# Second layer's scores as products of 64 rows, two heads in the two row halves of the array

## The chip, the cores and the metric

The kernel runs on one core of a Trainium2 chip. The metric is the device time of one execution in microseconds (us). The engines are TensorE (PE, its weight loads are PEld), VectorE (DVE), ScalarE (ACT), GpSimd (POOL) and SyncE (SP), which here only issues transfers.

## The reference

Two layers, each an attention over 77 context rows and a linear feed-forward, on x of 8 batches x 512 tokens x 512. What matters here is the attention of the second layer, with 16 heads of 64:

```python
q = jnp.einsum('bsd,dhe->bshe', inputs_q, Wq) + bq
k = jnp.einsum('bsd,dhe->bshe', inputs_kv, Wk) + bk
v = jnp.einsum('bsd,dhe->bshe', inputs_kv, Wv) + bv
q = q / jnp.sqrt(jnp.asarray(HD, dtype=q.dtype))
scores = jnp.einsum('bqhd,bkhd->bhqk', q, k)
weights = jax.nn.softmax(scores, axis=-1)
ctx = jnp.einsum('bhqk,bkhd->bqhd', weights, v)
out = jnp.einsum('bqhd,hde->bqe', ctx, Wo) + bo
```

with inputs_q the layer-normalised x (512 tokens), inputs_kv the context (77 rows), D = 512 and HD = 64. The first layer is alike with 16 heads of 32, a key mask and no output matrix. Its feed-forward has ternary weights and quantised rows; the second layer's is one real 512 x 512 matrix made in setup from two DFT products.

## The kernel before, in words

**Numbers.** Every operand of a product is held as a sum of two fp16 parts, high and low. `products` (L150 to L152) makes three matmuls of each product: high x high, high x low, low x high.

**Two programs.** `setup` (0 to about 191 us of the profile) scales and splits all weights and computes keys and values of all batches, which go to DRAM (`scr_k0`, `scr_v0`, `scr_k1`, `scr_v1`). The weights come through two staging buffers, `stage[:, 0]` and `stage[:, 1]`, filled by `load(i, n)` on the SP queue in the order of `STAGED`; each load waits until the weight before it in its buffer is split. VectorE runs a chain in one fixed order over them (`maximum`, `scaling`, `low`), among it the waits for `WO` and for `WV1A` and `WV1B`, the two halves of the second layer's value weights. Small vectors, the value bias `vb1` among them, are counted on one semaphore, `small_in`.

`layers` is one loop over steps i of 18 slots each; a step works on all four stages of neighbouring batches. W and X are the query projection, attention and feed-forward of the first layer, Y the second layer's query projection and attention, Z its output product and feed-forward: `("X", u)` and `("Y", u)` in `UNITS` are the eight score units of a batch and a layer. A unit is 128 tokens x 8 heads. `FILLS` says which other products ("fills": projections `q`, probabilities x values `pv`, output `out`, feed-forward `f`) TensorE makes in each slot into one of four banks `wb`. TensorE's order is written out: in slot g it makes the scores of the unit of slot g + 1, then the fills of slot g (for Y's unit 0 the fills come first). So a step has Y units 0 and 1 back to back; 2 behind a few fills; 3, 4 and 5 back to back, as two slots between them have no fills; then 6 and 7, each behind fills. Behind unit 5 stands the first projection of the next batch, `("W", "q", 0)`, 12 matmuls of 512 columns.

**A score unit's way.** Scores go to `sc[:, U % 2]`, two banks of 4 heads x 77 columns; units alternate between two pairs of banks. VectorE takes the maxima (L1135, `maxima`). In the units of `HEADWISE` ScalarE makes the exponentials head by head from the bank (L981, eight heads of 0.42 us and less); in the others VectorE subtracts the maxima (L1143) and ScalarE makes one pass (L985). GpSimd normalises, ScalarE and VectorE split into high and low (L994, L1155), and a transposing DMA on the SP queue turns the probabilities for `pv`. TensorE waits before unit U until the exponentials (or the subtraction) of unit U - 2 are done (L1210 and on, `scores`).

**Y's scores.** Queries of two heads, 2 x 64 rows, are one 128-row stationary operand `qc[:, h, pair, tok]`. The keys `k1b[rows, h, pair, j, :]` hold head j of the pair in rows 64 j to 64 j + 63 and zeros in the other half, so that one matmul over 128 rows and 2 x 77 = 154 columns gives both heads: the zeros take out the other head's rows. A unit is 4 pairs x 3 = 12 such matmuls. The one matmul of another row count in the loop is `ones` x `mrow` (L1223), one row, which adds the mask in every bank of an X unit.

Of the kernel before, what the change touches and what calls it, by code (L numbers as in the profile page):

```python
# [13 lines left out]
P = 128  # L14
B, S, D = 8, 512, 512
KEYS = 77
ROWS = B * KEYS
NT = S // P
ND = D // P
H0, H1 = 32, 64  # L20
D1 = 16 * H1
ND1 = D1 // P
# [208 lines left out]
def setup(nc, k, ctxT, wk0, bk0, wv0, bv0, wk1, bk1, wv1, bv1, scr_k0, scr_k1, scr_v0, scr_v1,  # L231
# [4 lines left out]
    with here:  # L236
# [3 lines left out]
        def sem(name):  # L240
            return here.enter_context(nc.semaphore(name))

        stage = sb("a_stage", [P, 2, ND * ROWS], F32)
# [40 lines left out]
        STAGED = [[("WF", wf[:, 0:ND * D], ND * D), ("WQ0", wq0, ND * D), ("WK0", wk0, ND * D), ("WK1A", wk1[:, :, 0:D], ND * D),  # L284
                   ("WV1B", wv1[:, :, D:D1], ND * D)],
                  [("WF", wf[:, ND * D:2 * ND * D], ND * D), ("CTX", ctxT, ND * ROWS), ("WV0", wv0, ND * D),
                   ("WV1A", wv1[:, :, 0:D], ND * D), ("WK1B", wk1[:, :, D:D1], ND * D)]]
        W_PLACE = {"WK0": 0, "WV0": 1, "WK1A": 0, "WK1B": 1, "WV1A": 1, "WV1B": 0}
# [41 lines left out]
        def _(sp):  # L330
            def load(i, n):
                name, src, width = STAGED[i][n]
                if n:
                    sp.wait_ge(lo_done, split_count(STAGED[i][n - 1][0]))
                o = stage[:, i, 0:width]
                if len(src.shape) == 3:
                    o = o.rearrange("p (c n) -> p c n", c=ND)
                sp.dma_start(o, src).then_inc(loaded[i], 16)
# [12 lines left out]
            sp.dma_start(vb0, bv0.partition_broadcast(P)).then_inc(small_in, 16)  # L351
            sp.dma_start(vb1, bv1.partition_broadcast(P)).then_inc(small_in, 16)
            sp.dma_start(k["bo"][:, :], bo.partition_broadcast(P)).then_inc(small_in, 16)
# [6 lines left out]
            sp.wait_ge(tern_full, ND)  # L360
            sp.dma_start(wo_ks[:, 0:ND1 * D], wo).then_inc(wo_in, 16)
            load(1, 2)
# [28 lines left out]
        def _(dve):  # L391
            step = Chain(dve, dve_step)

            arrival = {name: (loaded[i], 16 * (n + 1)) for i in range(2) for n, (name, _, _) in enumerate(STAGED[i])}
            arrival["WQ1"], arrival["WO"] = (wq1_in, 16), (wo_in, 16)
            biased = {"WQ0": k["bq0"], "WQ1": k["bq1"]}
# [118 lines left out]
            ternary()  # L515
            dve.wait_ge(small_in, 16 * 11)
            mask_rows()
# [89 lines left out]
        def _(act):  # L607
# [44 lines left out]
            for name in ("WK0", "WO", "WV0"):  # L652
                high(name)
            act.wait_ge(small_in, 16 * 11)
            k_factor(S_WK0, 0)
# [86 lines left out]
def layers(nc, k, x, scr_k0, scr_k1, scr_v0, scr_v1, out):  # L742

    here = ExitStack()
    with here:
# [437 lines left out]
        def _(pe):  # L1183
# [21 lines left out]
            def scores(stage, u, b):  # L1205
# [12 lines left out]
                tok = slice(t * P, (t + 1) * P)  # L1218
                for gg in range(2):
                    g = 2 * half + gg  # L1220
                    if stage == "X":
                        o = sc[:, U % 2, gg, 0:GK]
                        pe.matmul(o.rearrange("p (h n) -> p h n", h=4), ones[:, :], mrow[:, :, :].broadcast_to([1, 4, KEYS]), start=True, stop=False)  # L1223
                        ins = products(pe, o, lambda h: q0T[:, h, g, tok],
                                       lambda h: k0b[:, h, g, :, :].rearrange("p j n -> p (j n)"), False, True)
                    else:
                        for e in range(2):
                            pair = 2 * g + e
                            ins = products(pe, sc[:, U % 2, gg, e * 2 * KEYS:(e + 1) * 2 * KEYS], lambda h: qc[:, h, pair, tok],
                                           lambda h: k1b[:, h, pair, :, :].rearrange("p j n -> p (j n)"), e == 0, True, skip=True)  # L1230
                ins.then_inc(scores_full, 1)
# [149 lines left out]
```

## Time and profile before

| | |
|---|---|
| median of 3 runs | 1251.98 us (1246.87 to 1256.07) |
| the profiled execution: its own time | 1256.17 us |
| its span, first to last instruction | 1254.4 us |
| outside the span | 1.8 us |
| mean granted TensorE clock | 0.886 of full speed |
| TensorE matmuls busy | 998.0 us (80%) |
| VectorE busy | 959.6 us (77%) |
| ScalarE busy | 647.3 us (52%) |
| GpSimd busy | 401.0 us (32%) |

Setup takes the first 191 us or so, the loop the rest; a step in the middle of the loop takes about 115 us. Busy time of TensorE is the union of its matmuls, which overlap in the record, as each is drawn from its start to its end: the distance between two starts is what a matmul costs the engine, not its length. Idle time in brackets stands before an instruction, with what ended it.

### The profile page before, as it was taken

To read this page: it belongs to the slowest core of one execution; us is meant where nothing else is said; L and a number is where in the kernel's file an instruction comes from. 1 tells how busy PE (TensorE), PEld (TensorE's weight loads), DVE (VectorE), ACT (ScalarE), POOL (GpSimd) and SP (SyncE) were. 2 spreads that over 40 slices of the span, in tenths; PEclk is the share of its full clock that TensorE was granted. 3 is DMA by queue.
4 is the path that set the end of the run, shared out by engine and by line. 5 is a ranking of instruction groups with operands and counts; after the bars stand their busy time and mean duration, and the time that the engine had idled before them with its cause. 6 is when DMAs were issued, how large, how long until landed. Compare 5 with 4: busy or idle time off the path is not lost. (4 is left out here: it accounts for less than half of the span.)

```text
span 1254.4 us, 17113 instructions
## 1 busy us (share of the span) xinstructions
PE 998.0 (80%) x6020; PEld 501.3 (40%) x6020; DVE 959.6 (77%) x1740; ACT 647.3 (52%) x1658; POOL 401.0 (32%) x350
## 2 busy tenths in 40 slices
PE   3989940555686896899699969979996999589694
PEld 1446430232253344445344534444453445334341
DVE  5798874286879969987897899699979977954832
ACT  1334340353657637753864686377539645713701
POOL 0011004041433324523441444245234413521402
PEclk9999975756688799999799989998998999799797
DMA  8402232153555655665657555756755573560512
GB/s 336 167 34 76 108 118 91 34 128 68 89 115 101 106 103 98 116 128 105 109 103 154 82 115 102 139 98 120 128 109 111 97 128 69 95 119 17 100 52 67
DMA packets 374983, 132.83 MB, mean 106 GB/s; under 512 B 364753, under 2 KB 367345, under 8 KB 371442
## 3 DMA queue, kind: packets, MB, share of 16 engines
q1 hardware_dynamic: 374898, 131.74, 49.4%
q8 instruction: 48, 0.79, 0.3%
q14 instruction: 37, 0.30, 0.1%
HBM read 35.91 MB, written 16.11 MB: 41 GB/s over the span
## 5 line engine op out<-in xcount | busy, mean ns | idle before, releaser
L938 POOL TENSOR_TENSOR pr<-pr,sm 128x616 f32<-128x616 f32 x128 | 168.7, 1318 | 454.5 <-DVE sm L1150 454.5
L981 ACT ACTIVATE pr<-scores,mx,factor 128x77 f32<-128x77 f32 x512 | 204.3, 421 | 44.8 <-DVE mx L1138 44.8
L150 PE MATMUL wb<-xT,wq_hl 128*128 128x512 f16 x384 | 150.9, 393 | 68.4 <-DMA xT<-xh 68.4
L151 PE MATMUL wb<-xT,wq_hl 128*128 128x512 f16 x384 | 150.4, 392 | 0.0
L152 PE MATMUL wb<-xT,wq_hl 128*128 128x512 f16 x384 | 149.8, 390 | 0.0
L994 ACT ACTIVATE ph<-pr 128x618 f16<-128x618 f32 x128 | 92.8, 725 | 99.4 <-DMA prT<-ph 86.7
L150 PE MATMUL scores<-k1b,qc 128*128 128x154 f16 x256 | 62.0, 259 | 90.3 <-ACT pr L981 89.5
L1155 DVE SCALAR_TENSOR_TENSOR ph<-pr,ph 128x618 f16<-128x618 f32 x128 | 130.0, 1016 | 4.4 <-ACT ph L994 4.4
L929 POOL TENSOR_TENSOR rstd<-var,mhalf 128x2 f32<-128x2 f32 (+1 forms) x48 | 52.5, 1094 | 183.9 <-DVE var L1052 176.4
L981 ACT ACTIVATION_READ_ACCUMULATOR pr<-scores,mx,factor 128x1 f32 x512 | 107.9, 211 | 0.0
L1135 DVE TENSOR_REDUCE mx<-scores 128x8 f32<-128x616 f32 x128 | 101.3, 791 | 8.2 <-PE scores L152 8.2
L150 PE MATMUL wb<-wo_hl,qc 128*128 128x512 f16 x256 | 97.0, 379 | 3.0 <-DVE qc L1085 3.0
L152 PE MATMUL wb<-wo_hl,qc 128*128 128x512 f16 x256 | 97.0, 379 | 0.0
L151 PE MATMUL wb<-wo_hl,qc 128*128 128x512 f16 x256 | 97.0, 379 | 0.0
L1094 DVE SCALAR_TENSOR_TENSOR xr<-wb,factor,xr 128x512 f32<-128x512 f32 x48 | 35.8, 745 | 77.6 <-PE wb L152 77.6
L1078 DVE TENSOR_TENSOR xh<-xn,xh 128x1024 f16<-128x1024 f32 x48 | 73.4, 1530 | 25.1 <-ACT xn L1009 24.6
L1006 ACT ACTIVATE xh<-xr,shift,rstd 128x512 f16<-128x512 f32 x72 | 58.0, 814 | 56.2 <-POOL shift L931 33.6
L962 ACT ACTIVATE qc<-wb,bq_s 128x512 f16<-128x512 f32 x64 | 42.5, 688 | 82.6 <-PE wb L152 82.6
L150 PEld LDWEIGHTS wb<-xT,wq_hl 128*128 128x128 f16 x384 | 38.8, 101 | 114.1 <-issue 74.5
L1009 ACT ACTIVATE xn<-xr,shift,rstd 128x512 f32<-128x512 f32 x84 | 67.0, 812 | 11.6 <-POOL shift L931 10.3
L944 POOL TENSOR_TENSOR xr<-xr,bf_b 128x512 f32<-128x512 f32 x48 | 70.4, 1487 | 3.8 <-ACT xn L1009 3.8
L388 POOL PARTITION_ALL_REDUCE a_allmax<-a_absmax x16 | 15.9, 992 | 162.8 <-DVE a_absmax L406 94.1
(177 smaller groups left out, 2616.2 us busy)
## 6 DMA issues: line engine op xcount, KB each, us to landing
xr<-in_x SPq DMA_DIRECT2D x6, 1024.0 KB, 5.6
out_x<-xr SPq DMA_DIRECT2D x6, 1024.0 KB, 5.5
a_dft_kf<-in_dft SPq DMA_DIRECT2D x1, 3072.0 KB, 14.3
a_stage<-in_wk SPq DMA_DIRECT2D x3, 1024.0 KB, 5.6
a_stage<-in_wv SPq DMA_DIRECT2D x3, 1024.0 KB, 5.6
scr_v<-a_wq_vs SPq DMA_DIRECT2D x1, 2560.0 KB, 7.8
scr_k<-a_wo_ks SPq DMA_DIRECT2D x1, 2464.0 KB, 7.2
k1b<-scr_k SPq DMA_DIRECT2D x16, 154.0 KB, 6.7
```

Of the source, the lines that this page charges most:

```text
L150: pe.matmul(out, lhs(0), rhs(0), start=start, stop=False, **kw)
L151: pe.matmul(out, lhs(0), rhs(1), start=False, stop=False, **kw)
L152: return pe.matmul(out, lhs(1), rhs(0), start=False, stop=stop, **kw)
L938: pool.tensor_tensor(v, v, s, ALU.mult).then_inc(probs_ready, 1)
L944: ins = pool.tensor_tensor(xs(b)[:, t, :], xs(b)[:, t, :], k[bias][:, :], ALU.add)
L981: ins = act.activation(pr[U % 3][:, h // 4, cols], sc[:, U % 2, h // 4, cols], ACT.Exp, bias=mx[:, U % 4, h:h + 1], scale=k["factor"][:, f ...
L994: act.activation(ph[:, U % 2, 0, :, :, 0:CH], pr[U % 3][:, :, 0:GKP].rearrange("p g (c n) -> p g c n", c=3), ACT.Copy, scale=PS).then_inc( ...
L1006: ins = act.activation(xh[:, n % 2, t - pair, 0, :], xs(b)[:, t, :], ACT.Identity, bias=shift[:, j, t:t + 1], scale=rstd[:, j, t:t + 1])
L1009: ins = act.activation(xn[:, t - pair, :], xs(b)[:, t, :], ACT.Identity, bias=shift[:, j, t:t + 1], scale=rstd[:, j, t:t + 1])
L1078: dve.tensor_tensor(xh[:, n % 2, :, 1, :], xn[:, :, :], xh[:, n % 2, :, 0, :], ALU.subtract).then_inc(ln_lowered, 1)
L1135: step(dve.tensor_reduce(m, s, AX.X, ALU.max))
L1155: dve.scalar_tensor_tensor(out=ph[:, U % 2, 1, :, :, 0:CH], in0=pr[U % 3][:, :, 0:GKP].rearrange("p g (c n) -> p g c n", c=3), scalar=PS, ...
```

## The change

Y's scores become 24 matmuls of 64 rows and 77 columns a unit. A new argument `tile_position=(r * 64, 0)` puts the product in row half r of the array; the two halves hold different heads, and r = 0 and r = 1 write to two banks. The zero half of `k1b` is no longer read. A bank then holds four heads that are not four in a row in the old numbering, so values and output weights have to come in the same new order: `WV1A`, `WV1B` and the bias `vb1` are loaded in 8 pieces each in place of 1, and `WO` in 8 in place of 1, with the counts of the semaphores to match. All else in the loop stays as it is; nothing changes in the order of work on VectorE, ScalarE and GpSimd.

```diff
@@ setup: STAGED
-                   ("WV1B", wv1[:, :, D:D1], ND * D)],
+                   ("WV1B", wv1, ND * D)],
...
-                   ("WV1A", wv1[:, :, 0:D], ND * D), ("WK1B", wk1[:, :, D:D1], ND * D)]]
+                   ("WV1A", wv1, ND * D), ("WK1B", wk1[:, :, D:D1], ND * D)]]
@@ load
+                if name in ("WV1A", "WV1B"):
+                    a = name == "WV1B"
+                    o = o.rearrange("p (c b g r d) -> p c b g r d", c=ND, b=2, g=2, r=2)
+                    src = src.rearrange("p c (b r g a d) -> p c b r g a d", b=2, r=2, g=2, a=2)
+                    for b, g, r in itertools.product(range(2), range(2), range(2)):
+                        sp.dma_start(o[:, :, b, g, r, :], src[:, :, b, r, g, int(a), :]).then_inc(loaded[i], 16)
+                    return
@@ SP queue
-            sp.dma_start(vb1, bv1.partition_broadcast(P)).then_inc(small_in, 16)
+            vb1_v = vb1.rearrange("p (a b g r d) -> p a b g r d", a=2, b=2, g=2, r=2)
+            bv1_v = bv1.rearrange("(b r g a d) -> b r g a d", b=2, r=2, g=2, a=2)
+            for q, r in itertools.product(range(4), range(2)):
+                sp.dma_start(vb1_v[:, q // 2, q % 2, :, r, :], bv1_v[q % 2, r, :, q // 2, :].partition_broadcast(P)).then_inc(small_in, 16)
...
-            sp.dma_start(wo_ks[:, 0:ND1 * D], wo).then_inc(wo_in, 16)
+            wo_v = wo_ks[:, 0:ND1 * D].rearrange("p (f r e n) -> p f r e n", f=2, r=2, e=2)
+            wo_s = wo.rearrange("p (f e u n) -> p f e u n", f=2, e=2, u=2)
+            for f, r, u in itertools.product(range(2), range(2), range(2)):
+                sp.dma_start(wo_v[u * H1:(u + 1) * H1, f, r, :, :], wo_s[r * H1:(r + 1) * H1, f, :, u, :]).then_inc(wo_in, 16)
@@ VectorE of setup (ScalarE alike)
-            dve.wait_ge(small_in, 16 * 11)
+            dve.wait_ge(small_in, 16 * 18)
@@ TensorE: scores
-                    else:
-                        for e in range(2):
-                            pair = 2 * g + e
-                            ins = products(pe, sc[:, U % 2, gg, e * 2 * KEYS:(e + 1) * 2 * KEYS], lambda h: qc[:, h, pair, tok],
-                                           lambda h: k1b[:, h, pair, :, :].rearrange("p j n -> p (j n)"), e == 0, True, skip=True)
+                else:
+                    for q in range(4):
+                        for n, (h, h1) in enumerate(((0, 0), (0, 1), (1, 0))):
+                            for r in range(2):
+                                rows = slice(r * H1, (r + 1) * H1)
+                                ins = pe.matmul(sc[:, U % 2, r, q * KEYS:(q + 1) * KEYS], qc[rows, h, 4 * half + q, tok],
+                                                k1b[rows, h1, 4 * half + q, r, :], start=q == 0 and n == 0, stop=n == 2,
+                                                skip_group_check=True, tile_position=(r * H1, 0))
                 ins.then_inc(scores_full, 1)
```

On TensorE, in a middle step, the end of the back-to-back units 3, 4 and 5 and the start of the next batch's projection read before (the last 6 of 36 products of scores):

```order
2676 L150 MATMUL scores<-k1b,qc 128x154
2677 L151 MATMUL scores<-k1b,qc 128x154
2678 L152 MATMUL scores<-k1b,qc 128x154
2679 L150 MATMUL scores<-k1b,qc 128x154
2680 L151 MATMUL scores<-k1b,qc 128x154
2681 L152 MATMUL scores<-k1b,qc 128x154
2682 L150 MATMUL wb<-xT,wq_hl 128x512
2683 L151 MATMUL wb<-xT,wq_hl 128x512
```

and after the change, at the same place:

```order
2429 L1297 MATMUL wb<-tern,qiT 128x512 x4
2430 L1247 MATMUL scores<-k1b,qc 128x77 x72
2431 L151 MATMUL wb<-xT,wq_hl 128x512
2432 L152 MATMUL wb<-xT,wq_hl 128x512
2433 L153 MATMUL wb<-xT,wq_hl 128x512
```

Nothing has moved: 36 products of 154 columns are now 72 of 77, between the same neighbours (helper lines shift by one).

On the SP queue, in setup, from the load of `WK0` to that of `WK1B` before:

```order
19 L338 DMA a_stage<-in_wk 128x2048
20 L361 DMA a_wo_ks<-in_wo 128x4096
21 L338 DMA a_stage<-in_wv 128x2048
22 L338 DMA a_stage<-in_wk 128x4x512
23 L338 DMA a_stage<-in_wv 128x4x512 x2
24 L338 DMA a_stage<-in_wk 128x4x512
```

and after:

```order
19 L346 DMA a_stage<-in_wk 128x2048
20 L375 DMA a_wo_ks<-in_wo 64x2x512 x8
21 L346 DMA a_stage<-in_wv 128x2048
22 L346 DMA a_stage<-in_wk 128x4x512
23 L342 DMA a_stage<-in_wv 128x4x64 x16
24 L346 DMA a_stage<-in_wk 128x4x512
```

The one load of `WO` is 8, the two of `WV1A` and `WV1B` are 16, with runs of 64 values in place of 512, ahead of `WK1B`. At the start of the queue the load of `vb1` is 8 pieces of 128x2x64 in the same way, ahead of three more small loads.

## Rows read from the trace of the kernel before

**Rows 1.** The page, part 1: busy time, share, instructions

```profile
PE 998.0 (80%) x6020; PEld 501.3 (40%) x6020; DVE 959.6 (77%) x1740; ACT 647.3 (52%) x1658; POOL 401.0 (32%) x350
```

**Rows 2.** Busy time by stretch, then granted clock, DMA share, GB/s

```profile
736.00:850.00 114.00, 101.06 (x657) 51.30 (x655) 99.50 (x191) 72.39 (x199) 46.62 (x40) 0.95 0.60 115
729.00:735.00 6.00, 1.72 (x12) 1.41 (x12) 5.82 (x12) 5.67 (x22) 2.04 (x2) 0.50 0.95 181
735.00:739.00 4.00, 3.71 (x19) 2.37 (x20) 3.90 (x7) 4.00 (x8) 1.55 (x1) 0.55 0.69 135
```

**Rows 3.** Groups by form: count, then busy us, mean ns, idle before

```profile
L150 PE MATMUL scores<-k1b,qc 128*128 128x154 f16 x256 | 62.0, 259 | 90.3 <-ACT pr L981 89.5 <-DVE pr L1143 0.8
...
L152 PEld LDWEIGHTS scores<-k1b,qc 128*128 128x128 f16 x256 | 28.5, 111 | 0.0
```

**Rows 4.** Time line of TensorE, first and last Y block on the path

```profile
390.27 0.31 PE L150 MATMUL scores<-k1b,qc 128*128 128x154 f16 x1 [3.47 <-ACT pr L981]
...
1158.56 0.24 PE L150 MATMUL scores<-k1b,qc 128*128 128x154 f16 x1
```

**Rows 5.** Time line of TensorE, a Y unit at the high clock

```profile
717.82 0.24 PE L150 MATMUL scores<-k1b,qc 128*128 128x154 f16 x1 [1.31 <-ACT pr L981]
...
718.64 0.38 PE L150 MATMUL wb<-xT,wq_hl 128*128 128x512 f16 x1
```

**Rows 6.** Time line of TensorE, a Y unit at the low clock

```profile
735.29 0.31 PE L150 MATMUL scores<-k1b,qc 128*128 128x154 f16 x1 [3.92 <-ACT pr L981]
...
736.81 0.63 PE L150 MATMUL wb<-xT,wq_hl 128*128 128x512 f16 x1
```

**Rows 7.** Time line of TensorE round a product of one row

```profile
639.79 0.38 PE L152 MATMUL wb<-xT,wq_hl 128*128 128x512 f16 x1
640.11 0.30 PE L1223 MATMUL scores<-mrow,ones 1*128 1x308 bf16 x1
640.34 0.30 PE L150 MATMUL scores<-k0b,q0T 128*128 128x308 f16 x1
640.48 0.29 PE L151 MATMUL scores<-k0b,q0T 128*128 128x308 f16 x1
```

**Rows 8.** Time line of TensorE, products of 64 columns

```profile
599.71 0.19 PE L151 MATMUL wb<-v0b,prT 103*128 103x64 f16 x1
599.74 0.19 PE L152 MATMUL wb<-v0b,prT 103*128 103x64 f16 x1
```

**Rows 9.** Time line of TensorE, two more waits for the exponentials

```profile
729.66 0.31 PE L150 MATMUL scores<-k1b,qc 128*128 128x154 f16 x1 [6.60 <-ACT pr L981]
...
764.25 0.30 PE L1223 MATMUL scores<-mrow,ones 1*128 1x308 bf16 x1 [1.13 <-ACT pr L981]
```

**Rows 10.** Time line of ScalarE after the unit of Rows 6

```profile
740.48 0.69 ACT L962 ACTIVATE q0T<-wb,bq_s 128x512 f16<-128x512 f32 x1 [1.04 <-PE wb L152]
...
760.91 0.42 ACT L981 ACTIVATE pr<-scores,mx,factor 128x77 f32<-128x77 f32 x1 [1.46 <-DVE mx L1138]
```

**Rows 11.** Time line of VectorE in the same stretch

```profile
741.20 0.75 DVE L1087 SCALAR_TENSOR_TENSOR q0T<-wb,bq_s,q0T 128x512 f16<-128x512 f32 x1 [0.70 <-ACT q0T L962]
...
759.64 0.79 DVE L1135 TENSOR_REDUCE mx<-scores 128x8 f32<-128x616 f32 x1
```

**Rows 12.** Time line of the SP queue: loads of WO and of WV1A

```profile
44.45 0.43 SPq L361 DMA_DIRECT2D a_wo_ks<-in_wo  x1
...
93.82 0.56 SPq L338 DMA_DIRECT2D a_stage<-in_wv  x1
```

**Rows 13.** Time line of VectorE where setup needs these loads

```profile
33.12 1.09 DVE L468 COPY tern<-a_vbank 128x512 bf16<-128x512 bf16 x3 [4.01 <-PE a_vbank L706]
...
72.05 2.28 DVE L413 TENSOR_REDUCE a_parts<-a_wo_ks 128x1 f32<-128x2048 f32 x1
...
112.03 2.28 DVE L406 TENSOR_REDUCE a_absmax<-a_stage 128x1 f32<-128x2048 f32 x1
```

**Rows 14.** The view of DMA: KB each, median us from issue to landing

```profile
k1b<-scr_k SPq DMA_DIRECT2D x16, 154.0 KB, 6.7
```

More of the change, by code:

```diff
@@ L1 @@
+import itertools
 import numpy as np
@@ L392, in _ @@
             step = Chain(dve, dve_step)
-            arrival = {name: (loaded[i], 16 * (n + 1)) for i in range(2) for n, (name, _, _) in enumerate(STAGED[i])}
-            arrival["WQ1"], arrival["WO"] = (wq1_in, 16), (wo_in, 16)
+            parts_of = {"WV1A": 8, "WV1B": 8}
+            arrival = {name: (loaded[i], 16 * sum(parts_of.get(v[0], 1) for v in STAGED[i][:n + 1]))
+                       for i in range(2) for n, (name, _, _) in enumerate(STAGED[i])}
+            arrival["WQ1"], arrival["WO"] = (wq1_in, 16), (wo_in, 128)
             biased = {"WQ0": k["bq0"], "WQ1": k["bq1"]}
@@ L653, in _ @@
                 high(name)
-            act.wait_ge(small_in, 16 * 11)
+            act.wait_ge(small_in, 16 * 18)
             k_factor(S_WK0, 0)
@@ L1218, in scores @@
                 tok = slice(t * P, (t + 1) * P)
-                for gg in range(2):
-                    g = 2 * half + gg
-                    if stage == "X":
+                if stage == "X":
+                    for gg in range(2):
+                        g = 2 * half + gg
                         o = sc[:, U % 2, gg, 0:GK]
```

## Prediction

> **What bounds the kernel now.** I read the page first: TensorE 80% busy, VectorE 77%, so neither is idle enough to ignore [rows 1]. Next the stretches. A middle step of the loop, 736 to 850 us, has TensorE busy 101 of 114 us and VectorE 99.5 [rows 2]; what TensorE does not use is a few waits for the exponentials: 1.31 us before Y unit 2 [rows 5], 6.60 before unit 4 [rows 9], 3.92 before unit 5 [rows 6], 1.13 before an X unit at 764.25 [rows 9].
>
> To see what a shorter Y unit is worth I followed the waits back from the last instruction, at each start asking whether the engine's own instruction before it or a releaser was later. In a middle step the path runs so: VectorE and ScalarE, nearly without a pause, until unit 3's exponentials end and release unit 5 at 735.29; TensorE makes unit 5 and the projection behind it; that projection's end releases ScalarE at 740.48 [rows 10], which releases VectorE at 741.20 [rows 11]; VectorE works on until the maxima at 759.64 [rows 11], which release ScalarE's exponentials at 760.91 [rows 10], and these TensorE at 764.25; then TensorE alone for some 60 us, with no Y unit until units 0 and 1. Of the eight Y units of a step, one lies on the path: unit 5. Units 0 to 3 end in the idle time of 1.31 and 6.60 us, unit 4 starts at 729.66 and ends within that idle time, which lasts up to 735.29, and units 6 and 7 run beside VectorE's stretch and have 1.13 us of slack at 764.25.
>
> Over the whole run the path has 11 blocks of Y scores, first at 390.27 and last at 1158.56 [rows 4]: five single units at the low clock (one of them unit 5 above) and six blocks at the high clock, one of them double, so seven units there.
>
> **What a unit costs now.** High clock: 717.82 to 718.64, 0.82 us [rows 5], 0.068 for each of 12. Low clock: 735.29 to 736.81, 1.52 us [rows 6], 0.127 each. The granted clock is 0.50 in 729 to 735 and 0.55 in 735 to 739 [rows 2]: the engine had been idle for 6.60 and 3.92 us with one unit between [rows 6, 9], and the full clock came back shortly before 739. All second-layer scores together are 3 x 256 matmuls [rows 3].
>
> **What it costs after, full clock.** 24 matmuls. If they ran one after another, a matmul of 77 columns would take half of 0.068, 0.034. If halves run side by side, a pair takes 0.034, so 0.017 each. No row shows side-by-side products. The nearest row for how fast the engine can start matmuls that each have their own weights is the 64-column one: 0.030 from start to start [rows 8]; it may be the columns that set this and not the starts, so it is an upper bound for a floor. I take 0.029 each, nearest to that row, 24 x 0.029 = 0.70; ends 0.41 (all side by side, no floor) and 0.83 (nothing side by side).
>
> **The change of row count.** Where a one-row product stands between 128-row ones, the next start comes 0.23 us later, where 308 columns need 0.14 (the row below it); ahead of it, the start behind the 512-column matmul comes 0.32 us later, where 0.14 x 512 / 308 = 0.23 would do [rows 7]. So each change of shape costs 0.09, say 0.10 us at the high clock. Units of 64 rows between products of 128 rows change shape twice a block; I take 0.10 for each, with 0 as the lower end since a one-row product may be special, and 0.15 at the low clock. Entering after a wait is free, as the array is empty.
>
> What the row shows, the Trainium skill states as a rule: "Mode switching requires drain" (TensorEngine Tiling (Array Packing), Tiling Modes, Key Properties). The same page, under Performance Considerations, Instruction Overhead, speaks against this change: it gives some 60 cycles as the least time of a matmul and advises against taking a tiling factor from a dimension already small. By that figure, an estimate from the page, 24 starts at 25 ns are 0.60 us, and with two switches 0.80 against 0.82: nothing gained at the high clock. The result is the same as mine within 0.1 us a unit.
>
> **Sum, path blocks.** High clock: before 7 x 0.82 = 5.7 us; after 7 x 0.70 + 6 x 0.20 = 6.1: +0.4. Low clock: the columns bound, 0.127 / 2 / 2 = 0.032 each side by side, 24 x 0.032 = 0.77, plus 0.12 on leaving, 0.89 against 1.52: 0.63 saved in each of five. But behind it the same low clock still runs: if it rises at the same moment as before, only half of what is saved in low-clock time comes out, 0.31. So -1.6 to -3.2. Together -1.2 to -2.8; I take -2.
>
> **Units off the path** cost nothing: at 0.90 us a unit they differ from now by less than 0.1, against slacks of 1.13, 1.31 and 6.60. VectorE reads two whole banks as before, and its maxima start after other work, so an earlier end of a unit moves nothing.
>
> **Setup loads.** WV1A: 8 issues of 0.56 [rows 12] are 4.5 us of the SP queue, and 4,096 runs of 256 bytes. The nearest row is a pair of key loads, 2,048 runs of 154 bytes, that lands in 6.7 us [rows 14]; twice that is 13.4, so it lands by 93.8 + 0.6 + 13.4 = 107.8. VectorE asks for it at 112.03 [rows 13]: hidden by 4 us. WV1B has the same size and comes later in VectorE's chain, with more work ahead of it; WK1B's load behind it waits for a later split anyway. WO: 8 issues of 0.56 from 44.45 [rows 12] and runs of 2 KB, asked for at 72.05 [rows 13], 27 us after the first issue: hidden. The bias: 7 more issues of 0.56 push the last small load back by 3.9 us; VectorE waits for TensorE for 4.01 us right behind the place that needs it [rows 13]. I price all of setup at 0, at most 3 us.
>
> **Base.** The sum is made against the profiled execution: 1254.4 of span, 1256.17 in all, minus 2 is 1254.2. That execution is 4.2 us over the median of 1251.98; the same -2 on the median gives **1250**.
>
> **Rivals.**
> - Full overlap: halves side by side and no floor. High clock 7 x 0.41 + 1.2 - 5.7 = -1.6, low clock as above, and free switches another -1: -3 to -6, 1247.5. For it: 64-column matmuls run at about their columns' rate, 0.068 x 64 / 154 = 0.028 against 0.030 [rows 8], so no floor has shown yet. Chance 0.16.
> - It does not do what it says: the halves take turns. High clock 7 x 0.83 + 1.2 - 5.7 = +1.3; low clock 24 x 0.064 + 0.12 - 1.52 = +0.14, five times +0.7. +2, 1254. For it: no row with overlap. Chance 0.17.
> - Slower: weight loads stop hiding. A load lasts 0.111 us in the record [rows 3] and is hidden now, one beside another product. If a half's load can't go ahead of the other half's product, a unit is 24 x 0.11 = 2.6 us. In a step, unit 5 is +1.1; 6 and 7 together +3.6 less 1.13 of slack, +2.5; units 0 to 3 add 7.2, swallowed by 1.31 + 6.60. That is +3.6 a step, seven steps +25, and about +7 in the last step's bare blocks: 1284. It decides from about 0.06 us a matmul, where units 6 and 7 use up their slack. Against it: 64-column products load weights for each at 0.030 [rows 8]. Chance 0.09.
> - The clock: TensorE does less in the Y section, and the low clock lasts longer. It was low for some 3.6 us behind 735 (0.55 over 4 us [rows 2]); as much again at half speed costs 1.8 us a step, seven times +12: 1262. Against it: from 735.29 on TensorE has unbroken work either way. Chance 0.08.
> - Setup not hidden: +3, 1253. Chance 0.05.
>
> My forecast has 0.42, and 0.03 is left for a gain I don't see.
>
> **How the numbers follow.** Forecast, full overlap, taking turns and setup lie between 1244 and 1256 with a few us of spread between runs (1246.87 to 1256.07 before). The range is 1242 to 1263: it takes in most of the clock case and leaves out the weight loads. Measurement tells about 1% (12.5 us) from nothing. Slower by over 1%, past 1264.5: weight loads 0.09 and some of the clock case, 0.13. Faster, below 1239.5: 0.07. The rest, 0.80.
>
> **What would show each step.** In the profile after: starts of the 24 matmuls 0.029 apart at the high clock (0.017: full overlap; 0.034: taking turns; over 0.06: weight loads), 0.032 at the low clock; about 0.1 us more before the first 128-row product behind a block; unit 5 some 0.9 us long; the wait before an X unit near 764 still about 1 us; VectorE's maximum of WV1A with no wait for a transfer; the step still 114 to 115 us. I am wrong if the path has many more Y units than I found, or if a block of 64-row products changes what the clock does.

## The result, and the profile after

The changed kernel takes 1258.0 us (median of 20 runs, 1255.67 to 1262.26) against 1252.57 for the kernel before (20 runs, 1246.87 to 1256.29): ratio 1.0047, 95% interval 1.0036 to 1.0058. It is some 5.5 us slower, where 2 us less was forecast. The profiled execution has a span of 1259.2 us, 4.8 more than before, and took 1260.96 in all; its mean granted clock is 0.871 (0.886 before). Both profiled executions are long ones of their kernel, 3.0 us (after) and 3.6 us (before, 1256.17) over the median, so what follows splits the 4.8 us between these two, and not the medians.

Page, part 1, of the changed kernel, to be read against [rows 1]:

```profile
PE 992.1 (79%) x6788; PEld 477.2 (38%) x6788; DVE 965.5 (77%) x1740; ACT 647.1 (51%) x1658; POOL 399.8 (32%) x350
```

TensorE is busy 6 us less than before, in a span 4.8 us longer. So the scores did get cheaper, and something waits more. The groups by form, against [rows 3]:

```profile
L1247 PE MATMUL scores<-k1b,qc 64*128 64x77 f16 x1536 | 44.8, 218 | 97.7 <-ACT pr L997 96.1 <-DVE pr L1159 1.5
L1247 PEld LDWEIGHTS scores<-k1b,qc 64*128 64x128 f16 x1536 | 36.6, 108 | 111.9 <-ACT pr L997 100.8 <-issue 8.5 <-DVE pr L1159 1.7
```

Three groups, each some 62 us busy (their products overlap), are now one of 44.8, for twice as many products.

**The unit itself.** Time line of TensorE in the changed kernel, units 4 and 5 at the low clock, then unit 6 at the high clock with the products ahead and behind, against [rows 6, 9]:

```profile
728.80 0.96 PE L1247 MATMUL scores<-k1b,qc 64*128 64x77 f16 x24 [5.98 <-ACT pr L997]
733.99 0.96 PE L1247 MATMUL scores<-k1b,qc 64*128 64x77 f16 x24 [4.23 <-ACT pr L997]
734.89 0.61 PE L151 MATMUL wb<-xT,wq_hl 128*128 128x512 f16 x1
...
738.20 0.38 PE L152 MATMUL wb<-xT,wq_hl 128*128 128x512 f16 x1
738.41 0.38 PE L153 MATMUL wb<-xT,wq_hl 128*128 128x512 f16 x1
738.72 0.60 PE L1247 MATMUL scores<-k1b,qc 64*128 64x77 f16 x24
739.26 1.90 PE L1297 MATMUL wb<-tern,qiT 128*128 128x512 bf16 x8
```

The halves do run side by side. At the high clock a unit is 0.54 us from its first start to the next product (738.72 to 739.26; a unit was 0.82), and the start into it comes 0.31 behind a 512-column product (738.41 to 738.72) where 0.21 is usual (738.20 to 738.41), so entering costs 0.10. At the low clock it is 0.90 (733.99 to 734.89) against 1.52.

**The waits.** Before unit 4 TensorE idles 5.98 us (6.60 before), before unit 5 4.23 (3.92). The wait before the first X unit behind them, 1.13 us at 764.25 before, is called the X wait from here on. Time line of TensorE from the X wait of the same step, to be read against the second row of [rows 9]:

```profile
762.92 0.30 PE L1239 MATMUL scores<-mrow,ones 1*128 1x308 bf16 x1 [1.78 <-ACT pr L997]
...
764.29 0.39 PE L151 MATMUL wb<-m_hl,xT 128*128 128x512 f16 x1
764.51 0.60 PE L152 MATMUL wb<-m_hl,xT 128*128 128x512 f16 x1
764.90 0.63 PE L153 MATMUL wb<-m_hl,xT 128*128 128x512 f16 x1
765.33 0.63 PE L151 MATMUL wb<-m_hl,xT 128*128 128x512 f16 x1
...
768.67 0.30 PE L1239 MATMUL scores<-mrow,ones 1*128 1x308 bf16 x1
```

The wait has grown from 1.13 to 1.78 us, and 1.6 us after it ended the 512-column products turn from 0.22 us apart to 0.43: the low clock. From the first of these twelve to the next product it takes 4.38 us (764.29 to 768.67). In the kernel before it takes 2.69 for the same twelve, 1.69 less:

```profile
765.62 0.38 PE L150 MATMUL wb<-m_hl,xT 128*128 128x512 f16 x1
...
768.31 0.30 PE L1223 MATMUL scores<-mrow,ones 1*128 1x308 bf16 x1
```

The granted clock says the same. Busy time by stretch of the changed kernel, then granted clock; the first three answer to [rows 2]:

```profile
736.00:850.00 114.00, 100.15 (x730) 47.69 (x730) 99.44 (x188) 70.55 (x198) 46.20 (x40) 0.93 0.60 113
729.00:735.00 6.00, 1.77 (x49) 1.48 (x44) 5.79 (x14) 6.00 (x21) 1.66 (x1) 0.50 1.01 191
735.00:739.00 4.00, 4.00 (x28) 1.55 (x29) 3.57 (x8) 3.29 (x6) 2.87 (x3) 0.72 0.82 87
764.50:767.90 3.40, 3.40 (x10) 1.19 (x9) 3.37 (x6) 0.81 (x1) 2.08 (x3) 0.51 0.61 118
767.90:780.00 12.10, 12.10 (x60) 5.41 (x59) 11.18 (x19) 7.80 (x23) 2.43 (x2) 1.00 0.57 110
```

0.51 for 3.4 us behind the X wait and 1.00 from 767.9 on; the middle step has 0.93 where it had 0.95. The clock behind unit 5, where the prediction's rival on the clock looked, is no worse than before: 0.72 over 735 to 739 for a unit that starts 1.3 us earlier, and in both kernels the 512-column products are back at 0.22 apart some 3.3 us behind unit 5's start.

**The account.** Starts of unit 5 and of the first X unit, from the time lines of both kernels, cut the loop into legs. With "leg 5" from unit 5 to the X unit released by the wait, and "leg X" from there to unit 5 of the next step, over the five steps that begin at 503.75 before and at 502.10 after:

| us | before | after | difference |
|---|---|---|---|
| start to the first of these units 5 | 503.75 | 502.10 | -1.65 |
| leg 5, five times | 146.47 | 144.41 | -2.06 |
| leg X, five times | 423.95 | 430.82 | +6.87 |
| from the last unit 5 on | 180.22 | 181.87 | +1.65 |
| span | 1254.4 | 1259.2 | +4.8 |

The first row can't be put down to the scores: in e6, e1 and e10 (the runs of the next section), all with 128-row scores, this unit 5 starts at 500.30, 502.75 and 506.74. The loss is leg X. Four of the five grew by 1.7 us (85.28 to 86.98, 85.26 to 86.99, 85.26 to 87.00, 80.84 to 82.54). The other did not grow, 87.31 before and 87.32 after: the kernel before already loses this time once, behind a wait of 1.42 us. Its time line of TensorE and the stretch behind:

```profile
532.72 0.30 PE L1223 MATMUL scores<-mrow,ones 1*128 1x308 bf16 x1 [1.42 <-ACT pr L981]
```

```profile
533.80:537.20 3.40, 3.40 (x10) 1.37 (x9) 3.37 (x6) 0.81 (x1) 2.43 (x3) 0.50 0.51 97
```

### The profile page after: what moved, and what is told of

It reads as the page before. It is cut to its first block and busy times, and to the rows that moved or that the text cites. A ratio compares the mean times of both kernels' runs of the same rounds, so it can differ in the third digit from the quotient of the medians.

```text
span 1259.2 us, 18677 instructions
## 1 busy us (share of the span) xinstructions
PE 992.1 (79%) x6788; PEld 477.2 (38%) x6788; DVE 965.5 (77%) x1740; ACT 647.1 (51%) x1658; POOL 399.8 (32%) x350
## 5 line engine op out<-in xcount | busy, mean ns | idle before, releaser
L151 PE MATMUL wb<-xT,wq_hl 128*128 128x512 f16 x384 | 154.6, 403 | 68.0 <-DMA xT<-xh 68.0
L152 PE MATMUL wb<-xT,wq_hl 128*128 128x512 f16 x384 | 153.7, 400 | 0.0
L153 PE MATMUL wb<-xT,wq_hl 128*128 128x512 f16 x384 | 152.3, 397 | 0.0
L1171 DVE SCALAR_TENSOR_TENSOR ph<-pr,ph 128x618 f16<-128x618 f32 x128 | 133.2, 1041 | 5.1 <-ACT ph L1010 5.1
L1247 PE MATMUL scores<-k1b,qc 64*128 64x77 f16 x1536 | 44.8, 218 | 97.7 <-ACT pr L997 96.1
L1247 PEld LDWEIGHTS scores<-k1b,qc 64*128 64x128 f16 x1536 | 36.6, 108 | 111.9 <-ACT pr L997 100.8
```

Source lines behind the costliest of these rows:

```text
L151: pe.matmul(out, lhs(0), rhs(0), start=start, stop=False, **kw)
L152: pe.matmul(out, lhs(0), rhs(1), start=False, stop=False, **kw)
L153: return pe.matmul(out, lhs(1), rhs(0), start=False, stop=stop, **kw)
L1171: dve.scalar_tensor_tensor(out=ph[:, U % 2, 1, :, :, 0:CH], in0=pr[U % 3][:, :, 0:GKP].rearrange("p g (c n) -> p g c n", c=3), scalar=PS, ...
L1247: ins = pe.matmul(sc[:, U % 2, r, q * KEYS:(q + 1) * KEYS], qc[rows, h, 4 * half + q, tok], k1b[rows, h1, 4 * half + q, r, :], start=q == ...
```

## Experiments

**Theory A**: shorter Y units bring TensorE earlier to the X wait; the longer wait is followed by 3.4 us of low clock on a stretch that TensorE alone sets. **Theory B** is the rival that each expectation sets against it: the loads, or the 64-row products themselves (there also called rival C). Where no other kernel is named, ratios are to the kernel before.

**e1: the loads alone.** The kernel before with the new loads of WV1A, WV1B, vb1 and WO, scores as they were. Heads of scores and values no longer match in it.

```diff
-                   ("WV1B", wv1[:, :, D:D1], ND * D)],
+                   ("WV1B", wv1, ND * D)],
...
+                    for b, g, r in itertools.product(range(2), range(2), range(2)):
+                        sp.dma_start(o[:, :, b, g, r, :], src[:, :, b, r, g, int(a), :]).then_inc(loaded[i], 16)
```

> Only the loads are changed (pieces of WV1A, WV1B, WO and the bias), the scores are the old products of 128 rows; heads and values then don't match, so the output's heads are mixed, with the same work done. Theory A (the clock): in the changed kernel the path loses its time behind one wait for exponentials: with shorter score units TensorE idles 1.78 us there, not 1.13, the granted clock then falls for some 3.4 us once more in each step, and this costs 1.7 us in four steps or more; the loads cost nothing. It expects the time of the kernel before, 1252 us within 2. Theory B (the loads): smaller pieces cost time in setup or disturb the loop. It expects the changed kernel's 1258. In the profile A expects no low clock behind the waits near 764 and 832 us and a step of 114 to 115 us.

Measured 1254.45 us (1250.14 to 1256.31, 12 runs), ratio 1.0003, 0.9988 to 1.0017. That is 0.45 us over the 1252 ± 2 put down for it, and 1.5 over the kernel before as measured beside it (1252.95), with an interval that takes in no difference. Its five X waits are 0.87 to 1.19 us, none with a low clock behind it. The loads cost nothing that can be measured. The changed kernel's own rows show why, SP queue and VectorE:

```profile
93.02 5.90 SPq L342 DMA_DIRECT2D a_stage<-in_wv  x8
```

```profile
111.23 2.28 DVE L422 TENSOR_REDUCE a_absmax<-a_stage 128x1 f32<-128x2048 f32 x1
```

The eight issues take 5.9 us (4.5 estimated) and VectorE's maximum of WV1A has no wait ahead of it.

**e2: halves in turn.** All 12 products of half 0, then all 12 of half 1; the same work with little overlap.

```diff
-                    for q in range(4):
-                        for n, (h, h1) in enumerate(((0, 0), (0, 1), (1, 0))):
-                            for r in range(2):
+                    for r in range(2):
+                        for q in range(4):
+                            for n, (h, h1) in enumerate(((0, 0), (0, 1), (1, 0))):
```

> All of the change, but in a unit the 12 products of row half 0 come first and then the 12 of half 1; output unchanged. If halves overlap only where neighbours in the order lie in different halves, starts are 0.034 us apart and a unit takes 0.83 us and two changes of shape, 1.0 in all, 0.4 us longer than in the changed kernel. Theory A (the clock) expects that the longer units shrink the wait near 763 us to 1.1 us or less, that the low clock behind it goes, and that the total falls although the scores take longer: 1250 to 1255 us. The rival C, that the shape itself (changes between row counts, double the number of matmuls) costs the time, expects it to rise: some 1260 us or more, since 14 units on the path get 0.4 us longer each.

Measured 1256.8 us (1252.59 to 1259.77, 12 runs), ratio 1.0030, 1.0015 to 1.0046. Time line of TensorE:

```profile
716.82 0.90 PE L1247 MATMUL scores<-k1b,qc 64*128 64x77 f16 x24 [1.39 <-ACT pr L997]
717.66 0.39 PE L151 MATMUL wb<-xT,wq_hl 128*128 128x512 f16 x1
...
763.26 0.30 PE L1239 MATMUL scores<-mrow,ones 1*128 1x308 bf16 x1 [0.86 <-ACT pr L997]
```

0.84 us a unit (716.82 to 717.66), where halves side by side take 0.54 at the same clock: the order of the products alone decides it. The five X waits are 0.74 to 0.86, no low clock follows, and leg X is back at 422.35 in sum. So 64-row products by themselves, where they take as long as the old ones, bring no low clock behind the X wait. So far as expected. But the time came out 1.8 us over the 1250 to 1255 that I had put down (and under the rival's 1260), and the profile says where: leg 5 sums to 149.42, 3 us over the kernel before. One of them, with the stretch behind its start:

```profile
618.72 1.47 PE L1247 MATMUL scores<-k1b,qc 64*128 64x77 f16 x24 [4.17 <-ACT pr L997]
...
649.01 0.30 PE L1239 MATMUL scores<-mrow,ones 1*128 1x308 bf16 x1 [0.74 <-ACT pr L997]
```

```profile
618.70:622.00 3.30, 3.28 (x29) 2.01 (x30) 3.27 (x6) 3.30 (x5) 1.12 (x1) 0.50 1.03 99
622.00:625.10 3.10, 3.10 (x9) 0.88 (x6) 1.53 (x4) 0.86 (x2) 3.10 (x4) 0.50 0.38 93
```

Here the low clock that begins ahead of unit 4 lasts until 6.4 us behind unit 5's start, and leg 5 is 30.29 us. The section on the prediction takes this up.

**e3: more work on the path.** Three useless products of 512 columns in front of the X wait of the changed kernel, in the first feed-forward sum of each batch.

```diff
                 pe.wait_ge(*rows_of(3, t - t % 2, b))
+                if t == 0:
+                    products(pe, o, lambda h: xT4[:, t, h, 0, :], lambda h: k["m"][:, h, 0, :], True, True)
```

> The changed kernel with three useless matmuls of 512 columns, 0.65 us, ahead of the wait near 763 us of each step (the first three products of one feed-forward fill are made twice); output unchanged. Theory A (the clock): the wait shrinks from 1.78 to 1.13 us, the low clock behind it goes in the four steps that have it alone, 4 x 1.7 = 6.8 us less: 1250 to 1253 us, below the changed kernel and near or below the one before. Rival C (shape or instructions cost the time): useless work can't help, 1258 or up to 5 us more, as 0.65 us a step is added.

Measured 1254.38 us (1247.05 to 1256.33, 12 runs), ratio 1.0008, 0.9991 to 1.0025: 3.6 us under the changed kernel by adding work, with intervals that don't meet, though 1.4 over the 1250 to 1253 put down. Time line of TensorE, and the stretch behind the wait:

```profile
756.17 0.30 PE L1239 MATMUL scores<-mrow,ones 1*128 1x308 bf16 x1 [1.14 <-ACT pr L997]
```

```profile
757.50:761.00 3.50, 3.50 (x19) 1.44 (x17) 3.47 (x6) 0.81 (x1) 2.31 (x3) 1.00 0.59 112
```

The five waits are 0.39 to 1.15 us, the clock behind them is full, leg X sums to 422.34 (430.82).

**e4: more work off the path.** The same three products ahead of the wait before Y unit 2, in the changed kernel.

```diff
+                if stage == "Y" and m == 6:
+                    products(pe, o, lambda h: w[:, h, 0, m * P:(m + 1) * P], lambda h: xT[:, :, h, 0, :], True, True)
```

> The same three useless matmuls (0.65 us), but in a projection fill ahead of the wait before Y unit 2, near 716 us, where the low clock also comes once more in each step but a wait of 5.98 us follows on TensorE. Output unchanged. Theory A: the low clock there goes too, but as the stretch is off the path the time stays, 1258 within 2 us (and the wait before unit 4 gets back to about 6.6). A cruder theory D, that each extra low stretch costs its 1.7 us wherever it stands, expects five times 1.7 less: 1250.

Measured 1257.13 us (1255.99 to 1261.78, 9 runs), ratio 1.0041, 1.0025 to 1.0057. Time line of TensorE:

```profile
714.83 0.60 PE L1249 MATMUL scores<-k1b,qc 64*128 64x77 f16 x24 [1.21 <-ACT pr L997]
715.37 0.39 PE L151 MATMUL wb<-xT,wq_hl 128*128 128x512 f16 x1
...
761.27 0.30 PE L1241 MATMUL scores<-mrow,ones 1*128 1x308 bf16 x1 [1.75 <-ACT pr L997]
```

The wait before unit 2 fell from 1.85 to 1.21 us and the low clock behind it is gone (715.37 follows after 0.54 us), and the median is 0.9 us under the changed kernel's, with intervals that overlap: the wait before unit 4 takes the gain up, 7.14 us where I had expected 6.6. So taking the low clock behind unit 2 away gained nothing. That it is the place alone and not the amount is not shown here, as the low clock round units 4 and 5 is longer in return, 13.7 us (from 722.0) where the changed kernel has 10.2 (from 727.0). Of the five X waits the three of 1.67 to 1.75 us keep their low clock, and two, 1.04 and 1.59, have none; its profiled execution, the fastest of its nine, is 5 us shorter than that of the changed kernel.

**e5: less work in the kernel before.** The 128-row kernel with three of the twelve products in front of the X wait left out (a quarter of one feed-forward sum per batch).

```diff
-                for c in range(ND):
+                for c in range(1 if t == 0 else 0, ND):
```

> The kernel before with three products of 512 columns, 0.65 us a step, left out of the same feed-forward fill ahead of the wait near 764 us (so one quarter of that sum is missing in the output for a quarter of the tokens). No 64-row products anywhere. Theory A (the clock): the wait grows from 1.13 to 1.78 us, the granted clock falls behind it in every step, and the kernel gets slower by doing less: 1256 to 1259 us. Rival C (shape or number of matmuls makes the changed kernel slow): 1252 or a little below.

Measured 1257.26 us (1255.13 to 1261.08, 8 runs), ratio 1.0046, 1.0027 to 1.0065: the changed kernel's loss, with no 64-row product in it and 0.65 us less work a step. Time line of TensorE and the stretch behind:

```profile
763.52 0.30 PE L1223 MATMUL scores<-mrow,ones 1*128 1x308 bf16 x1 [1.74 <-ACT pr L981]
...
765.41 0.63 PE L152 MATMUL wb<-m_hl,xT 128*128 128x512 f16 x1
765.83 0.63 PE L150 MATMUL wb<-m_hl,xT 128*128 128x512 f16 x1
```

```profile
765.20:768.50 3.30, 3.30 (x10) 1.18 (x9) 3.27 (x6) 0.81 (x1) 1.98 (x3) 0.51 0.63 122
```

Of its waits of 2.02, 1.51, 1.74, 1.64 and 1.56 us three have the low clock behind them, and those legs X are 1.7 us longer. This run decides for theory A: it needs nothing of the change but its shorter work. With e2, which has the 64-row products and neither the shorter work nor the low clock, it also answers the thought that the products' shape brings the low clock.

**e6: e3's products in the kernel before.** The partner of e3, same edit, so that both have the full clock behind the X wait.

> The kernel before with the three useless products of 512 columns ahead of the wait near 764 us. Output unchanged. Theory A: the wait goes from 1.13 to some 0.5 us; of the steps before one in seven had a low clock behind it, so 0 to 2 us less, 1250 to 1253. It also tells what the 64-row scores are worth once the clock is the same on both sides: the changed kernel with this padding took 1254.4, and my sum of parts has it 2 us below this one.

Measured 1254.43 us (1247.75 to 1256.65, 12 runs), ratio 1.0012, 0.9995 to 1.0029; waits 0.22 to 0.73 us. It was put down at 1250 to 1253. Against e3's 1254.38: with the clock behind the X wait alike, 64-row scores are worth nothing that can be measured, where I had expected 2 us.

**e7, e8: TensorE kept busy through the Y section.** Unit 3 and unit 4 are repeated to fill the waits before units 4 and 5: 17 and 10 times in the changed kernel (e7), 8 and 5 times in the one before (e8), beside both paddings of e3 and e4.

```diff
-                    for q in range(4):
+                    for q in [q for _ in range({3: 17, 4: 10}.get(u, 1)) for q in range(4)]:
```

> The changed kernel with useless work in all waits of the Y section: both paddings of 0.65 us, the products of Y unit 3 made 17 times over and of unit 4 ten times (7 and 4 us a step, both in waits of 6 and 4 us; output unchanged). Theory A: TensorE is never idle for long before unit 5, so the low clock of 10 to 14 us in each step goes too; it now lasts 3 to 5 us past the start of unit 5 on the path, which costs half of that, 1.5 to 2.5 us in some seven steps. It expects 1236 to 1246 us. Rival C expects more than 1258, as 11 us a step are added.

> The same for the kernel before: both paddings, unit 3 made 8 times and unit 4 five times (6.6 and 4.1 us), 128-row products, output unchanged. Theory A: as for the changed kernel, 1236 to 1246 us. With the clock high in both, the difference of this pair is what the 64-row scores save on the path, 0.4 us for unit 5 in seven steps: I expect this one 1 to 4 us above the other.

e7 measured 1298.02 us (1293.87 to 1312.2, 6 runs), ratio 1.038, 1.0339 to 1.0421, far from the 1236 to 1246 that theory A put down. Its time line of TensorE in units 3 to 5:

```profile
618.95 2.44 PE L1249 MATMUL scores<-k1b,qc 64*128 64x77 f16 x128 [1.18 <-issue]
622.67 2.44 PE L1249 MATMUL scores<-k1b,qc 64*128 64x77 f16 x128 [1.29 <-issue]
627.60 2.45 PE L1249 MATMUL scores<-k1b,qc 64*128 64x77 f16 x128 [2.48 <-issue]
631.33 0.56 PE L1249 MATMUL scores<-k1b,qc 64*128 64x77 f16 x21 [1.27 <-issue]
```

Behind the first 267 of the small products, and from there on behind every 128, stands a gap, here of 1.2 to 2.5 us, put down to "issue", not to any engine. The filling became the bound: unit 5 (631.33) no longer waits for exponentials. So the time is over rival C's 1258 too, for a reason that is neither theory's, and the run doesn't tell them apart.

e8 measured 1255.12 us (1250.54 to 1257.19, 12 runs), ratio 1.0026, 1.0012 to 1.0039. It did what it was built for. Stretch from ahead of unit 4 to behind unit 5, and the time lines of TensorE and VectorE:

```profile
721.00:735.00 14.00, 11.99 (x113) 8.46 (x114) 13.36 (x24) 13.66 (x44) 7.59 (x6) 1.00 0.86 154
```

```profile
727.21 0.24 PE L150 MATMUL scores<-k1b,qc 128*128 128x154 f16 x1 [1.44 <-ACT pr L981]
...
756.01 0.30 PE L1225 MATMUL scores<-mrow,ones 1*128 1x308 bf16 x1 [1.33 <-ACT pr L981]
```

```profile
731.39 0.80 DVE L1149 TENSOR_REDUCE sm<-pr 128x8 f32<-128x616 f32 x1 [0.33 <-ACT pr L985]
732.22 0.20 DVE L1150 RECIPROCAL sm<-sm 128x8 f32<-128x8 f32 x1
732.34 0.70 DVE L1087 SCALAR_TENSOR_TENSOR q0T<-wb,bq_s,q0T 128x512 f16<-128x512 f32 x1
```

The clock is full all through, unit 5 and the projection behind it run at twice the speed, and leg 5 still is 28.80 us (727.21 to 756.01; the five are 28.80 to 29.04). VectorE now takes q0T without a pause, where it waited 0.70 us [rows 11]: it was about to be the late one anyway. The expected 1236 to 1246 was a miss here too: unit 5 is worth what stands between 28.8 and the leg of the kernel before, and no more.

**e9, e10: the padding without its cost at the end.** e3 and e6 carry the three products in the last two batches too, where no X wait follows.

```diff
-                if t == 0:
+                if t == 0 and b < B - 2:
```

> The changed kernel with the three useless products of 512 columns in front of the X wait, but only for batches 0 to 5: the last two batches, whose feed-forward no longer stands in front of such a wait, carry none. Output unchanged. In the padded kernel of the earlier run the last two cost 0.65 us (full clock) and about 1.3 us (half clock) on a stretch that TensorE alone sets. Theory A (what made the change slower is the clock behind the X waits and, in the last two batches, 1 us of half-clock products behind the bare score blocks): X waits stay at or under about 1.2 us, the legs behind them stay at 85.3 us, and the time is 2 us under the fully padded kernel: about 1252.4, level with the kernel before (ratio 0.998 to 1.002). Theory B (64-row products cost something more that the padding does not touch): the time stays at 1254 to 1255.

> The same three products, batches 0 to 5 alone, in the kernel before (128-row scores, old loads). Output unchanged. It is the partner of the run beside it: the same clock behind the X waits in both, so their difference is what 64-row scores are worth by themselves. Theory A, from the profiles of the two fully padded kernels: the legs from unit 5 to the X wait are 0 to 1 us each longer here where the half clock lasts over 4 us behind unit 5 (2 us over five steps), the last batches 1 us shorter: so 1252.4 to 1253.5, 0 to 1 us above its partner. If 64-row scores were worth the 3 to 6 us of the full-overlap rival, this kernel would be 3 us or more above its partner.

e9 (64 rows) measured 1254.0 us (1246.31 to 1258.03, 12 runs), ratio 1.0012, 0.9993 to 1.0030; e10 (128 rows) 1251.99 us (1246.42 to 1256.52, 12 runs), ratio 0.9995, 0.9977 to 1.0013. The intervals overlap. e10 lies 0.4 under the range put down for it, e9 1.6 over its 1252.4, at the lower end of the 1254 to 1255 that theory B had (64-row products cost something more), and the order of the two is the reverse of what I had expected. So a cost of 64-row scores of up to some 2 us, besides the clock behind the X wait, is not ruled out. No kernel here beats the one before.

## Why the prediction was wrong, by its own steps

**The step that failed: "Units off the path cost nothing: at 0.90 us a unit they differ from now by less than 0.1, against slacks of 1.13, 1.31 and 6.60."** The difference was larger. A full-clock unit and the product ahead of it take 0.85 us (738.41 to 739.26) where 0.21 + 0.82 = 1.03 was usual, so 0.18 less in each of units 6 and 7. Unit 5 is 0.62 shorter, of which more low clock in the projection behind it takes some 0.3 back: from unit 5's start to the product behind unit 6 it was 5.80 us (735.29 to 741.09) and is 5.27 (733.99 to 739.26). And I asked only whether a longer unit would use up the slack. They got shorter. From unit 5 to the X wait TensorE worked 28.96 - 1.13 = 27.83 us before and 28.93 - 1.78 = 27.15 after, 0.68 less; the slack grew by 0.65 us, and with the longer idle time there the low clock came onto leg X. Four steps at +1.7 us are 6.9 us, which gains elsewhere bring down to the 4.8 of the profile. e5 shows the same without the change, e3 takes it away.

Over eleven kernels (before, after, and all runs but e7), five X waits each: 40 waits of 0.22 to 1.34 us, none with a low clock behind it; 11 of 1.64 to 2.02 us, all with one; of four between (1.42, 1.51, 1.56, 1.59), the shortest alone. That is a count of what these kernels did at one place; it is no rule for another, and the length of the wait alone does not decide. Before Y unit 2 six kernels (the one before, e1, e2, e5, e6, e10) have a wait of 1.65 to 1.74 us with no low clock behind it, and of ten of 1.84 to 2.22 us in e3 and e9 six have it and four not. The longest of these, time line of TensorE in e3, with the stretch behind:

```profile
595.66 0.60 PE L1247 MATMUL scores<-k1b,qc 64*128 64x77 f16 x24 [2.22 <-ACT pr L997]
```

```profile
595.70:599.50 3.80, 3.75 (x39) 1.91 (x40) 3.33 (x10) 3.80 (x7) 1.22 (x1) 1.00 0.50 95
```

What else decides it no run here shows.

**The clock rival had the mechanism and the wrong wait.** It reads "TensorE does less in the Y section, and the low clock lasts longer", and was placed behind unit 5. The argument against it (unbroken work from 735.29 on) holds there, and I did not put the same question to the X wait. It was sized at 1.8 us a step, seven times; measured are 1.7 us in five, one of which the kernel before has too. The row at 532.72 was in the trace of before, with the low clock behind it and a leg X of 87.31 among others of 85.27. I had looked at one middle step.

**The floor of 0.029 us per product was wrong.** A row of 24 products is 0.60 us long and a row of 128 in e7 is 2.44, so each further one adds 1.84 / 104 = 0.0177 on average. Two products of 77 columns take the time of one (0.034, half of 0.068): full overlap. The pages "TensorEngine Tiling (Array Packing)" (Performance Considerations, Instruction Overhead) and "TensorE: Matmul & The Clock Gate" (Part 1) of the Trainium skill give a least time of some 60 cycles or 25 ns per matmul; these rows are below it, so the rule did not bind where two row halves take products in turn. The 0.030 of [rows 8] goes with its columns (0.068 x 64 / 154 = 0.028).

**The high-clock term, +0.4, was wrong with it.** With 0.54 us a unit and 0.10 for entering it is 7 x 0.54 + 6 x 0.10 = 4.4 against 5.7, a credit of 1.3. Where I can follow it, that credit did not reach the time either. In the last step two such units together take 0.96 us (1154.88 to 1155.84) where they took 1.61 (1151.63 to 1153.24), and the unit behind them, which had no wait [rows 4], then waits 0.52 for exponentials. Time line of TensorE in the changed kernel:

```profile
1161.71 0.60 PE L1247 MATMUL scores<-k1b,qc 64*128 64x77 f16 x24 [0.52 <-ACT pr L997]
```

**The shape change was right**: 0.10 us at the head of a block, and 0.54 - 24 x 0.0177 = 0.12 behind the last start. **The low-clock unit was right**: 0.90 us, forecast 0.89.

**The credit for it, -1.6 to -3.2, was mis-sized.** How long leg 5 is goes with how long the low clock lasts behind unit 5's start. Read in the ten kernels with a low clock there (e7 left out): up to 3.7 us, leg 5 is 28.79 to 28.97 whatever the scores. At 4.6 to 5.3 us it is 28.94 to 29.20 with halves side by side (e3, e4, e9), 29.36 to 29.63 with 128 rows and 29.74 in e2 (one leg of e6, at 4.3, is 29.17). At 5.9 to 6.4 it is 29.99 to 30.29 (128 rows, and e2; no kernel with halves side by side had one). So 0.62 us saved in unit 5 gives 0 to 0.15 in the first case, since VectorE and ScalarE are nearly late themselves, and some 0.4 to 0.5 in the second. Two of the five legs before were of the longer kinds; that makes about 1 us in all (an estimate). In the changed kernel all five happened to be of the first, hence -2.06, which is luck in part. This also is e2's 3 us: four of its five were long.

**The last two batches** cost 1.65 us that I had not priced. From one output product to the next, starts at 1117.97 and 1203.67 before, 1121.11 and 1207.79 after, it takes 85.70 and 86.68 us; e2, e4 and e9, all with 64-row scores, have 86.6 to 86.8, e1 and e10, with 128 rows, 85.6. The low clock takes in more of the 24 products behind the last bare score units. Time lines of TensorE, before and after:

```profile
1180.32 0.59 PE L150 MATMUL wb<-prT,v1b 103*128 103x512 f16 x1 [0.21 <-DMA prT<-ph]
...
1186.46 0.38 PE L150 MATMUL wb<-m_hl,xT 128*128 128x512 f16 x1
```

```profile
1183.10 0.59 PE L151 MATMUL wb<-prT,v1b 103*128 103x512 f16 x1 [0.88 <-DMA prT<-ph]
...
1190.58 0.38 PE L151 MATMUL wb<-m_hl,xT 128*128 128x512 f16 x1
```

6.14 us against 7.48. A further 0.7 us is the last 48 products (12.10 and 12.78 us), again in part at the low clock. What causes this is open. The idle time ahead has grown, 0.21 to 0.88 us, but in e2, whose units are no shorter than before, the same 24 products take 7.25 us too, and in e5, with 128 rows and 0.24 us of idle time, 7.37 (between the same starts). The loss shows in every trace with 64-row scores (e7 left out) and is offset in e9, whose leg from the last unit 5 to the first of these output products is 42.03 us where it is 43.77 in e10: from the last unit 5 to the end they take 180.01 and 180.00 us.

**Setup at 0 was right** (e1). **The signs together**: the sum came out at -2 because every term in it was the cost of work, and the term that decided was the cost of not working, which has no place in it.

**What stays open.** e3, e6, e9 and e10 make 64-row scores, with a full clock behind the X wait, between 0 and 2 us slower than 128-row ones by their medians, with intervals that overlap; the account above has about -1 in leg 5 and +1.65 at the end. Runs of one kernel differ by 5 us and more, and of the 20 of the changed kernel those at a mean clock of 0.871 took 1260.96 to 1262.26, those at 0.874 to 0.876 1255.67 to 1258.84. That the low clock lasts longer at some place in the former fits, and was not seen, as each kernel has one trace.

## What to carry to other kernels

Shortening an engine's work ahead of a wait that another engine ends gains nothing there and lengthens the wait; on TensorE, look at every such wait that has TensorE-bound work behind it, and at the granted clock behind the longest of them over all steps, before calling off-path savings free. The same slack can be used: three useless products (0.65 us) in front of the wait took 3.6 us off the changed kernel, which brings it level with the kernel before and not below it. And the gain of a faster piece on the path is at most the lateness of whoever comes next: here 0.15 us of 0.62.

## What was not expected of the hardware

Products of 64 rows in the two row halves, alternating, start 0.0177 us apart on average at 77 columns and full clock; the same 24 with the halves one after the other take 0.84 us a unit instead of 0.54. In long runs of such products, each with its own weights, gaps named "issue" stood in e7, in the rows shown 1.18 to 2.48 us behind 267 and then behind each 128 of them, and none within the blocks of 24 and 48 of the changed kernel. A half-clock stretch of 3.4 us followed each of eleven X waits of only 1.64 to 2.02 us, while before Y unit 2 waits of up to 2.22 us stayed without one.
